# GpSimd drains in the scatter loop of the expert tiles

## The chip, the cores and the metric

The kernel runs on one core of a Trainium2 chip. The metric is device time in microseconds (us) of one execution. The engines are named as the profile names them: PE (TensorE, with PEld for its weight loads), DVE (VectorE), ACT (ScalarE), POOL (GpSimd) and SP (SyncE, which here only issues DMAs). POOL also issues DMAs, and all those whose rows are chosen by a list of indices (DMA_INDIRECT) come from it.

## What is computed

The reference is one transformer layer on x of 4 x 1024 x 256 in f32: a layer norm, a causal attention, a second attention with 16 heads, and a feed-forward part with routed experts. The change is in the last part, which per token is

```python
h = _swiglu(flat @ W1_shared)
routed = jnp.zeros_like(shared)
for e in range(E):
    routed = routed + h @ W2_experts[e] * w[:, e:e + 1]
out = x + (shared + routed).reshape(Bb, Tt, C)
return _rmsnorm(out, norm2_w)
```

with 8 experts, of which w is non-zero for two per token (both of one group of four). The kernel's output is x plus the causal attention plus this.

## The kernel before

Four stages follow one another: `project`, `causal_attention`, `head_attention` and `feed_forward`. Each is a block in which every engine has its own program. At the end of a block each engine executes a DRAIN, then all meet at a barrier; semaphores are then cleared, with two more POOL drains and a barrier for each such clearing (lines 69 and 70). The DRAINs of the block ends stand in the trace under the line that opens the block: L296, L677, L1545 and, for `feed_forward`, L1938.

`feed_forward` has two parts. First come 8 chunks of 512 tokens: hidden values, gates, shared expert, and rows of all tokens written to DRAM (`hidden_d` with the hidden values, `rows_d` with hidden values, base and rest in rows of 1040 f32). In this part POOL sends the tokens to their places in the lists of the 12 pairs of experts, 4 indirect DMAs a chunk, so 32, and gathers the lists back with one more (L1159).

The second part, from some 1280 us to the end, works off 43 expert tiles of 128 tokens (`TILES`, line 31); the tokens of one tile have the same two experts. Tile t passes through these steps, each on its engine:

- POOL gathers its rows from `rows_d` into one of 8 slots (`gather`, L1957, recorded at L1960). For the first 6 tiles the hidden values are gathered once more ahead of that (`gather_early`, L1954), from `hidden_d`.
- PE turns it (`turn_tile`, L2114: 4 transposes), which waits for the gather's landing.
- ACT rounds it (`tile_high`, L2182), DVE takes the rest (`tile_low`, L2251).
- PE multiplies it by its two experts (`experts`, L2130: 24 matmuls).
- DVE adds the weighted sums to the base (`sums`, L2259), ACT squares (L2189) and takes the root (L2195), DVE scales and finishes (`final`, last instruction L2277, which raises `fin_done`).
- POOL scatters the 128 finished rows to the output (`scatter`, L1963, recorded at L1965), once `fin_done` is t + 1.

The order on each engine is written out by hand. PE runs turn(t + 1) ahead of experts(t). DVE runs, in step t: tile_low(t + 1), sums(t - 1), final(t - 2), mean_square(t - 1). So final(t - 3) stands behind tile_low(t), and tile_low(t) behind turn(t). POOL issues gathers 0 to 5, then

```python
for t in range(TILES):
    scatter(t)
    if t + AHEAD < TILES:
        gather(t + AHEAD)
```

with `AHEAD` = 6, so that gather(t + 6) stands behind scatter(t), and from t = 37 on there are only scatters. A gather into a slot that has been used waits for the landing of the scatter two tiles back (`out_sent`). After the loop POOL (L1994) and SP (L2061) wait for the landing of all scatters, and the block ends. Counted out of the program, POOL issues 32 + 1 + 6 + 43 + 43 = 125 DMAs in this block, 21 in the block before it and 38 in `causal_attention`; none in `project`.

Of the kernel before, what the change touches and what calls it, by code (L numbers as in the profile page):

```python
# [30 lines left out]
TILES = N // P + CLASSES - 1  # L31
# [53 lines left out]
class HeadInputs:  # L85
# [3 lines left out]
    RING = 3  # L89
    AHEAD = RING - 1  # L90
    LOADS = 2 * NT * SIDES
    PLACE = PAIRS * S * 4

    def __init__(self, nc, ctx, q_d, k_d, vh_d):
        self.dram = (q_d, k_d, vh_d)
        self.nc = nc
        base = -(-nc.sbuf_base // 32) * 32
        self.base, self.all = base, ctx.enter_context(nc.sbuf_tensor("h_place", [P, 2 * self.AHEAD * PAIRS * S], F32))
        assert nc.sbuf_base == base + 2 * self.AHEAD * self.PLACE
        at = lambda name, i, dt: nc.alloc_sbuf_tensor_at(name, [P, PAIRS, S], dt, offset=base + i * self.PLACE)  # L100
        self.q6 = [at(f"h_q{r}", 2 * r, F32R) for r in range(self.AHEAD)]
        self.k6 = [at(f"h_k{r}", 2 * r + 1, F32R) for r in range(self.AHEAD)]
        self.spares = [at(f"h_spare{i}", i, F32) for i in range(2 * self.AHEAD)]
        self.vh = []
# [1742 lines left out]
def feed_forward(nc, inputs, heads, ya_d, ffw, routing, rows_d, hidden_d, out):  # L1847
# [5 lines left out]
    with ExitStack() as ctx:  # L1853
# [84 lines left out]
        with nc.Block() as block:  # L1938

            @block.gpsimd  # L1940
            def _(pool):
                def whole_ya(c):
                    pool.wait_ge(routing.xn_in, (c + 1) * 16)
                    pool.wait_ge(ya_in[c % 2], (c // 2 + 1) * 16)
                    theirs = rows[c % 2][:, :, REST:REST + D]
                    nc.gpsimd.tensor_tensor(theirs, theirs, xn[:, :, :], ALU.add).then_inc(ya_whole, 1)

                def low_parts(c, i):
                    pool.wait_ge(h_rounded, c * KH + i + 1)
                    nc.gpsimd.tensor_tensor(h[LO][:, i, :], whole[i % 2], h[HI][:, i, :].bitcast(F32),  # L1950
                                            ALU.subtract).then_inc(h_split, 1)

                def gather_early(t):
                    pool.indirect_dma_start(early[t], None, hidden_d,  # L1954
                                            bass.IndirectOffsetOnAxis(listed[:, t:t + 1], 0)).then_inc(early_in[t], 16)

                def gather(t):  # L1957
                    if t >= SLOTS:
                        pool.wait_ge(out_sent[t % SLOTS], t // SLOTS * 16)
                    pool.indirect_dma_start(slot(t), None, rows_d, bass.IndirectOffsetOnAxis(listed[:, t:t + 1], 0))\  # L1960
                        .then_inc(row_in[t % SLOTS], 16)

                def scatter(t):  # L1963
                    pool.wait_ge(fin_done, t + 1)
                    pool.indirect_dma_start(out, bass.IndirectOffsetOnAxis(listed[:, t:t + 1], 0), base(t), None,  # L1965
                                            bounds_check=N - 1, oob_is_err=False).then_inc(out_sent[t % SLOTS], 16)

                for c in range(NCH):
                    routing.send(pool, c)
                    for i in range(KH):  # L1970
                        low_parts(c, i)
                        if i == 1 and c == LASTS:
                            routing.gather_lists(pool)
                    if WHOLE <= c + 1 < NCH:
                        whole_ya(c + 1)
                pool.wait_ge(*fills.released(("LISTS", 0)))
                pool.wait_ge(zeros_stored, 2 * 16)
                for s in range(2):
                    pool.wait_ge(hidden_stored[s], NCH * 16)
                for t in range(EARLY):  # L1980
                    if early[t] is whole[0]:
                        pool.wait_ge(h_split, NCH * KH)
                    gather_early(t)
                pool.wait_ge(rest_stored, NCH * 16)
                pool.wait_ge(rows_stored, NCH * 16)
                AHEAD = SLOTS - 2
                for t in range(AHEAD):
                    gather(t)
                for t in range(TILES):
                    scatter(t)  # L1990
                    if t + AHEAD < TILES:
                        gather(t + AHEAD)
                for s in range(SLOTS):
                    pool.wait_ge(out_sent[s], len(range(s, TILES, SLOTS)) * 16)  # L1994
# [409 lines left out]
```

## Time and profile before

| | |
|---|---|
| median of 3 runs | 1465.1 us (1464.88 to 1467.75) |
| profiled execution, its own time | 1463.6 us |
| its span, first to last instruction | 1461.9 us |
| mean granted TensorE clock | 0.972 |
| PE / DVE / ACT / POOL busy | 1380.3 / 1136.0 / 854.8 / 371.9 us |
| last scatter issued / span ends | 1450.0 / 1461.9 us |

The span is what the profile covers; 1.7 us of the execution lie outside it. Busy time is the time in which an engine executes instructions that the profile counts; a drain is a sequencer instruction and not counted as busy. In a row of the timeline the columns are start and duration in us, engine, line, operation, output<-inputs, shapes and count, and in brackets how long the engine had been idle and what released it.

### The profile page before, as it was taken

Reading aid. Unit: us, or ns where it says so; the run is one execution under the profiler, and the core shown is the slowest. Engines: PE = TensorE matmul, PEld = TensorE weight load, DVE = VectorE, ACT = ScalarE, POOL = GpSimd, SP = SyncE. Lnnn points to the kernel's source line nnn. Section 1 sums busy time; section 2 is a strip of 40 time slices with the busy share of each in tenths; the row PEclk is TensorE's granted clock in tenths of the full one; section 3 lists DMA queues with packets and bytes.
Section 4 is the critical chain, followed back from the end, with each engine's and each line's share of the span. In section 5 each row is a group of like instructions: output and inputs, shape, how many; then the busy total and the mean of one; then the engine's idle time right before and its main releaser. Section 6 shows DMA issues by size and latency. Waiting matters only on the chain. (4 is left out here: it accounts for less than half of the span.)

```text
span 1461.9 us, 26960 instructions
## 1 busy us (share of the span) xinstructions
PE 1380.3 (94%) x9749; PEld 816.1 (56%) x9749; DVE 1136.0 (78%) x1803; ACT 854.8 (58%) x1573; POOL 371.9 (25%) x368
## 2 busy tenths in 40 slices
PE   6999799979999999999999999989999999989995
PEld 3655577734333333333333333335888888789985
DVE  3786575588999999999999999924677776657764
ACT  2445443304888888888888888885334343323332
POOL 0344294045241000000000000101233333355553
PEclk9999999957999999999999999999999999999998
DMA  5799769351443344443322234213565654365551
GB/s 188 266 320 342 250 224 249 71 98 59 91 109 67 44 67 66 67 67 60 67 55 51 46 58 67 75 59 47 166 161 153 175 152 132 88 217 177 176 174 62
DMA packets 119746, 185.06 MB, mean 127 GB/s; under 512 B 26614, under 2 KB 74122, under 8 KB 119622
## 3 DMA queue, kind: packets, MB, share of 16 engines
q1 hardware_dynamic: 94341, 124.55, 34.6%
q0 software_dynamic: 14816, 45.19, 10.4%
q10 hardware_dynamic: 10464, 13.64, 3.1%
q8 instruction: 82, 1.34, 0.4%
q14 instruction: 43, 0.34, 0.1%
HBM read 102.36 MB, written 81.88 MB: 126 GB/s over the span
## 5 line engine op out<-in xcount | busy, mean ns | idle before, releaser
L1799 DVE TENSOR_REDUCE i_saT<-h_banks 128x2 f32<-128x1024 f32 x512 | 617.8, 1221 | 24.9 <-PE h_banks L1668 17.1
L1768 ACT ACTIVATE h_p<-h_banks 128x512 f32<-128x512 f32 x1024 | 551.2, 598 | 137.3 <-PE h_banks L1687 121.9
L1708 PE MATMUL h_po<-h_p,h_v 128*32 128x256 f32 (+1 forms) x3728 | 318.4, 413 | 3.5 <-ACT h_p L1768 1.4
L1687 PE MATMUL h_banks<-h_q,h_k 50*128 50x512 f32 x1024 | 254.4, 495 | 11.7 <-ACT h_p L1768 6.0
L1668 PE MATMUL h_banks<-h_k,h_q 48*128 48x512 f32 x1024 | 222.8, 431 | 10.7 <-DVE i_saT L1799 6.8
L1687 PEld LDWEIGHTS h_banks<-h_q,h_k 50*128 50x128 f32 x1024 | 95.8, 183 | 235.0 <-ACT h_p L1768 190.4
L1708 PEld LDWEIGHTS h_po<-h_p,h_v 128*32 128x32 f32 x3728 | 73.4, 108 | 170.7 <-issue 83.8
L2130 PE MATMUL f_ob<-w_experts,f_h 128*128 x1032 | 146.4, 291 | 1.3 <-issue 0.2
L2130 PEld LDWEIGHTS f_ob<-w_experts,f_h 128*128 128x128 f32 x1032 | 129.9, 191 | 10.3 <-issue 8.1
L1564 POOL COPY h_v<-h_values 128x512 f32<-128x512 f32 x14 | 8.6, 612 | 459.4 <-DMA h_values<-vh_d 459.4
L1668 PEld LDWEIGHTS h_banks<-h_k,h_q 48*128 48x128 f32 x1024 | 101.1, 194 | 38.4 <-DVE i_saT L1799 28.0
L2176 ACT ACTIVATE h_v<-f_pair 128x512 f32<-128x512 f32 x64 | 38.2, 597 | 131.2 <-PE f_pair L2079 131.1
L2079 PE MATMUL f_pair<-w_routed,r_x1p 128*128 128x512 f32 x384 | 93.7, 400 | 2.1 <-PEq L70 2.1
L2079 PE MATMUL f_pair<-r_x1p,w_shared 128*128 128x512 f32 x384 | 92.9, 396 | 2.3 <-DVE f_rows L2238 2.3
L2079 PEld LDWEIGHTS f_pair<-w_routed,r_x1p 128*128 128x128 f32 x384 | 72.6, 191 | 18.3 <-issue 3.0
L2079 PEld LDWEIGHTS f_pair<-r_x1p,w_shared 128*128 128x128 f32 x384 | 71.3, 187 | 19.8 <-DVE f_rows L2238 3.1
L2238 DVE TENSOR_TENSOR h_place<-h_v,f_pair 128x512 f32<-128x512 f32 x48 | 32.9, 686 | 50.1 <-ACT h_v L2176 49.8
L746 PE MATMUL a_sc<-c_kT,c_qT 128*128 128x512 f32 (+3 forms) x192 | 68.3, 493 | 2.3 <-PEq L296 2.3
L1950 POOL TENSOR_TENSOR f_h<-h_place,f_h 128x512 fp32r<-128x512 f32 x32 | 43.8, 1368 | 98.6 <-ACT f_h L2169 97.0
L2251 DVE TENSOR_TENSOR f_h<-f_pair,f_h 128x512 fp32r<-128x512 f32 x43 | 29.7, 692 | 49.0 <-ACT f_h L2182 49.0
L308 POOL TENSOR_TENSOR h_spare<-h_spare,t_sin 128x512 f32<-128x512 f32 x28 | 41.9, 1530 | 101.3 <-DVE h_spare L184 101.3
L773 PE MATMUL a_out<-a_v,a_pT 128*128 128x256 f32 x432 | 63.6, 298 | 0.0
(266 smaller groups left out, 1695.5 us busy)
## 6 DMA issues: line engine op xcount, KB each, us to landing
h_q<-q_d SPq DMA_DIRECT2D x84, 128.0 KB, 5.9
h_k<-k_d SPq DMA_DIRECT2D x84, 128.0 KB, 7.0
ot_d<-h_o ACTq DMA_DIRECT2D x32, 256.0 KB, 2.9
q_d<-t_parts SPq DMA_DIRECT2D x12, 512.0 KB, 5.0
k_d<-t_parts SPq DMA_DIRECT2D x12, 512.0 KB, 5.1
p_xin<-in_L_attn_x SPq DMA_DIRECT2D x8, 512.0 KB, 5.1
xn_d<-p_xn SPq DMA_DIRECT2D x8, 512.0 KB, 5.1
xnT_d<-p_xnT SPq DMA_DIRECT2D x8, 512.0 KB, 6.0
```

The costliest lines, as they stand in the source:

```text
L308: last = nc.gpsimd.tensor_tensor(swap[:, j, :], swap[:, j, :], sin[:, s, :], ALU.mult)
L746: ins = nc.tensor.matmul(sc[u % 2][:, c:c + w], qT[b % 2][:, k, i * P:(i + 1) * P], kT[b % 2][:, k, c:c + w], start=k == 0, stop=k == KD - 1)
L773: ins = nc.tensor.matmul(out[u % 2][:, 0:D], pT[u % 2][left][:, j, :], vp[b % 2][right][:, j, :], start=j == 0 and n == 0, stop=j == i and ...
L1668: ins = nc.tensor.matmul(bank_of(("SLOT", slot), g), q6[r][at, p, i * P:(i + 1) * P], k6[r][at, p, half * CH:(half + 1) * CH], start=True, ...
L1687: ins = nc.tensor.matmul(bank_of(key, g), k6[r][at, p, j * P:(j + 1) * P], q6[r][at, p, c * CH:(c + 1) * CH], start=True, stop=True)
L1708: ins = nc.tensor.matmul(po[h * VW:(h + 1) * VW, at], vh[n % RING][:, j, h, :], probs[u % PR][:, h, at], start=j == 0 and (part == 0 or la ...
L1768: nc.scalar.activation(probs[u % PR][:, h, :], bank_of(("PAIR", f // SIDES), f % SIDES), ACT.Exp, scale=DH ** -0.5).then_inc(exp_done, 1)
L1799: nc.vector.tensor_reduce(halfmax[n % 2][:, m, :], both_banks(("SLOT", slot)), AX.X, ALU.max)\
L1950: nc.gpsimd.tensor_tensor(h[LO][:, i, :], whole[i % 2], h[HI][:, i, :].bitcast(F32), ALU.subtract).then_inc(h_split, 1)
L2079: ins = nc.tensor.matmul(ps[:, half, :], left, right, start=n == 0, stop=n == len(terms) - 1)
L2130: ins = nc.tensor.matmul(to, h[left][:, t % KH, k * P:(k + 1) * P], w2s[right][:, bass.ds(e, 1), k, :], start=k == 0 and n == 0, stop=k == ...
L2176: nc.scalar.activation(sil[f % 2], fills.buffer(key)[:, 0, :], ACT.Silu).then_inc(sil_done[f % 2], 1)
```

## The change

Three lines are added to POOL's loop over the tiles. Ahead of the scatters of tiles 0, 4, 8, ..., 40 and of tile 42 POOL executes a drain: 12 in all. Nothing is removed or moved, and no other engine's program differs.

```diff
@@ -1984,9 +1984,12 @@
                 pool.wait_ge(rest_stored, NCH * 16)
                 pool.wait_ge(rows_stored, NCH * 16)
                 AHEAD = SLOTS - 2
+                DRAINED = 4
                 for t in range(AHEAD):
                     gather(t)
                 for t in range(TILES):
+                    if t % DRAINED == 0 or t == TILES - 1:
+                        pool.drain()
                     scatter(t)
                     if t + AHEAD < TILES:
                         gather(t + AHEAD)
```

## Rows read from the trace of the kernel before

**Rows 1.** Busy time by stretch: us, PE, PEld, DVE, ACT, POOL, PEclk, DMA share, GB/s.
```profile
1280.00:1290.00 10.00, 6.25 (x34) 5.68 (x33) 2.87 (x6) 1.20 (x2) 7.65 (x8) 0.69 0.72 219
...
1300.00:1440.00 140.00, 136.28 (x1056) 126.59 (x1054) 99.20 (x266) 48.74 (x153) 75.10 (x76) 1.00 0.54 172
```

**Rows 2.** Waits from 1300 to 1440 us: total us, times, longest.
```profile
PE f_pair L2114 <- DMA f_rows<-rows_d,r_listed: 2.3, 3, 1.2
```

**Rows 3.** Timeline, all engines, gather 6 to gather 9.
```profile
1301.58 0.98 POOL L1960 DMA_INDIRECT f_rows<-rows_d,r_listed  x1 [0.30 <-issue]
...
1305.72 0.66 PE L2114 MATMUL f_pair<-h_v,f_rows 128*128 128x128 f32 x4 [0.64 <-DMA f_rows<-rows_d,r_listed]
...
1306.52 0.58 ACT L2182 ACTIVATE f_h<-f_pair 128x512 fp32r<-128x512 f32 x1
...
1307.13 0.69 DVE L2251 TENSOR_TENSOR f_h<-f_pair,f_h 128x512 fp32r<-128x512 f32 x1 [0.75 <-ACT f_h L2182]
...
1307.74 0.99 DVE L2259 SCALAR_TENSOR_TENSOR f_rows<-f_ob,f_rows 128x256 f32<-128x256 f32 x2
...
1309.36 0.42 DVE L2277 TENSOR_TENSOR h_place<-h_place 128x256 f32<-128x256 f32 x1
...
1310.62 1.02 POOL L1965 DMA_INDIRECT out_dram<-h_place,r_listed  x1 [1.17 <-DVE h_place L2277]
...
1311.94 0.97 POOL L1960 DMA_INDIRECT h_place<-rows_d,r_listed  x1 [0.30 <-issue]
```

**Rows 4.** Line 1960, all 43 gathers: time from issue to landing.
```profile
DMA to landing us min/median/max: 4.1/4.3/6.9
```

**Rows 5.** Line 1965, all 43 scatters: time from issue to landing.
```profile
DMA to landing us min/median/max: 2.1/2.5/4.2
```

**Rows 6.** Timeline of POOL: gather 5, scatter 0, gather 42, scatters 39 to 42.
```profile
1293.84 0.94 POOL L1960 DMA_INDIRECT f_rows<-rows_d,r_listed  x1 [0.30 <-issue]
1300.23 1.04 POOL L1965 DMA_INDIRECT out_dram<-h_place,r_listed  x1 [5.44 <-DVE h_place L2277]
...
1434.07 0.97 POOL L1960 DMA_INDIRECT h_place<-rows_d,r_listed  x1 [0.30 <-issue]
...
1443.60 0.99 POOL L1965 DMA_INDIRECT out_dram<-f_rows,r_listed  x1 [2.69 <-DVE f_rows L2277]
1445.76 0.98 POOL L1965 DMA_INDIRECT out_dram<-h_place,r_listed  x1 [1.18 <-DVE h_place L2277]
1448.48 1.08 POOL L1965 DMA_INDIRECT out_dram<-h_place,r_listed  x1 [1.74 <-DVE h_place L2277]
1449.95 0.98 POOL L1965 DMA_INDIRECT out_dram<-h_place,r_listed  x1 [0.40 <-issue]
```

**Rows 7.** POOL's drains by line: ns min/median/max, first and last start us.
```profile
L1938 POOLq DRAIN  x1: 7978/7978/7978, 1452.4 to 1452.4; - x1
...
L1545 POOLq DRAIN  x1: 1775/1775/1775, 989.2 to 989.2; - x1
...
L677 POOLq DRAIN  x1: 3172/3172/3172, 269.1 to 269.1; - x1
...
L296 POOLq DRAIN  x1: 4799/4799/4799, 140.5 to 140.5; - x1
...
L69 POOLq DRAIN  x4: 93/118/218, 294.8 to 1461.3; - x4
...
L70 POOLq DRAIN  x4: 34/43/46, 295.7 to 1461.6; - x4
```

**Rows 8.** Packets of POOL's DMA queue: 148 to 270, 295 to 1000, 1003 to 1461 us.
```profile
q0 software_dynamic: 2784, 8.92, 29.6%
...
q0 software_dynamic: 2240, 7.55, 3.7%
...
q0 software_dynamic: 9792, 28.72, 19.6%
```

**Rows 9.** Timeline of POOL around the drain of L296.
```profile
139.24 5.95 POOL L308 TENSOR_TENSOR h_spare<-h_spare,t_sin 128x512 f32<-128x512 f32 x4 [10.32 <-DVE h_spare L184]
```

## The prediction

> **What bounds the kernel now.** I read the busy times by stretch first, then the waits of the tile stage, then the timeline of one turn of its loop, and last the drains. From 1300 to 1440 us PE is busy 136.28 of 140 us at the full 2.4 GHz level [rows 1]: the tile stage is PE's, so long as its tiles come in time. They come barely in time. The waits show that PE stood before a tile's transposes for a gather only 3 times for long, 2.3 us in all [rows 2], but that says nothing of the slack of the other tiles, and the timeline does. Gather 6 is issued at 1301.58 and its transposes wait for it until 1305.72. From there the reader can follow one turn of a loop [rows 3]: transposes of tile 6, ACT's rounding, DVE's tile_low(6), sums(4), final(3) ending at 1309.78, scatter(3) at 1310.62, gather(9) at 1311.94. That turn carries three tiles and takes 1311.94 - 1301.58 = 10.36 us when the gather is what ends it. From gather 6 to gather 42, 36 tiles take 1434.07 - 1301.58 = 132.5 us [rows 3, 6], so 3.68 us a tile and 11.04 for three. The loop through POOL is thus within 0.7 us per three tiles of being the bound itself. POOL is only half busy (75.10 of 140 us [rows 1]), yet whatever delays a scatter delays the gather behind it, and soon PE.
>
> The other place is the end. The last scatter is issued at 1449.95 and takes some 2.1 us to land, but the span goes on to 1461.9. Most of that is one instruction: POOL's drain of the block's end, 7.98 us from 1452.4 [rows 6, 7].
>
> **What a drain costs.** Three drains behind blocks with POOL DMAs took 3.17, 1.78 and 7.98 us, with 2784, 2240 and 9792 packets on POOL's queue in the blocks [rows 7, 8]: 1.1, 0.8 and 0.8 ns a packet, or 83, 85 and 64 ns a DMA at 38, 21 and 125 DMAs. It does not follow what lies further back, for the second is shorter than the first; and drains that follow another take 34 to 218 ns. So a drain goes through each DMA issued since the last one, though the program had waited for all of them beforehand. It also waits: the drain of L296, with no DMA before it, began at 140.5 behind queued POOL work and took 4.80 us, to 145.3, when that work had ended at 139.24 + 5.95 = 145.19 [rows 7, 9]; about 0.1 us after.
>
> What no row shows is a drain with DMAs in flight, and in the loop there are always some. The two ends: it returns at once for them (8 DMAs of 64 ns, 0.5 us, inside POOL's idle 1.17 us before a scatter [rows 3]), or it waits until the youngest has landed. I take the second. The nearest rows are these drains themselves: one waits for older work, and one that visits each DMA has little else to look for than whether it is done.
>
> **The sum.** One drain in the loop, ahead of scatter t: the youngest DMA is gather(t + 5). It lands 4.3 us after its issue at the median [rows 4], the drain ends 0.1 later, and then scatter(t) needs what it needs after any release: from the end of final(3), 1309.78, to the start of scatter(3), 0.84 us [rows 3]. Gather(t + 6) follows the scatter by 1.32 [rows 3]. Gather to gather: 4.3 + 0.1 + 0.84 + 1.32 = 6.6 us, where the pace was 3.68. POOL's earlier idle time is no cover, because the tiles that follow cannot make up the loss before the next drain: gather(t + 9), the youngest before drain t + 4, hangs on gather(t + 6) through the three-tile turn. That turn is 10.36 with a landing of about 4.1; with 4.3 it is 10.6. So four tiles take 6.6 + 10.6 = 17.2 us instead of 4 x 3.68 = 14.7: 2.5 us a drain. Between gather 6 and gather 42 lie nine such rounds (drains 4 to 36): +22.3 us.
>
> Drain 0 has some 45 DMAs to go through (about 3 us) and waits for gather 5: issued at 1293.84, landing up to 6.9 us later, 1300.7. Scatter 0 goes out at 1301.6 instead of 1300.23: +1.4 us [rows 4, 6], passed on at once because gather 6 was waited for. Drain 40 waits for scatter 39 alone; scatter 40 comes at least 2.1 + 0.1 + 0.84 = 3.1 us after it, where it was 2.16, and 0.9 us later is made good before scatter 41, 2.7 us on [rows 5, 6]. Drain 42 waits for scatter 41: 3.1 us instead of 1.47, +1.7 us that nothing behind it hides. The drain at the end then has one DMA to visit instead of 125: it falls from 7.98 to 0.2 us, a gain of 7.8. Nothing else is added: SP only waits for the landings, and the scatters themselves are the same.
>
> Together: 22.3 + 1.4 + 1.7 - 7.8 = **+17.6 us**. Against the profiled execution, 1463.6, that is 1481.2; the median of the runs lies 1.5 above it, so 1482.7, and I say 1482.5.
>
> The Trainium skill ("VectorE: DVE Perf Modes", section "The DRAIN you can't avoid") speaks of the drains of preamble and postamble as about 12 ns each, constant, on all engines. By that there would be no 7.8 us to gain and the sum would be some +25. The trace disagrees for POOL: 34 ns to 7.98 us [rows 7].
>
> **The range.** Downwards: the 0.84 us could be mostly sequencer work that overlaps the wait, as little as 0; 0.8 x 11 drains = 9 us less, 1473.5. Upwards: 0.5 us instead of 0.1 between landing and the drain's end adds 4.4 us; landings in the upper part of 4.1 to 6.9 add another few; and PE's gap of 2.5 us in each round may cost clock: from 1280 to 1290 PE was busy 6.25 of 10 us and the granted clock was 0.69, between the levels of 2.4 and 1.2 GHz [rows 1]. The transposes on the loop, 0.66 us, could at worst double, 6 us in nine rounds. Not all of these come together: 1492.
>
> **Rivals.** First, on the other side: the drain does not wait for DMAs in flight. Its price in the loop is then 0.5 us in POOL's idle 1.17, and nothing moves up to drain 42, which stands directly between scatters 41 and 42 and costs 0.2 to 0.5. The gain at the end stays: -7.8 + 0.4 = -7.4 us, 1457.7. The point that decides is drain 4: does it end before or after gather 9 has landed? For it speaks that every drain of the trace found its DMAs done, so that going through them may be bookkeeping only; against it, the drain that waited for older work. A rule of the Trainium skill points this way ("Perfetto Trace Analysis", section "DMA Instruction — SWDGE (GPSIMD)"): an indirect DMA's record ends when the last descriptor is written, not when the data has moved, and a drain that waits for older instructions would be done with it there. No row here shows whether a drain holds to that. I give it 0.11.
>
> Second: the drain waits as I say, but the end keeps its 7.98 us, because what is gone through are all DMAs of the block and not those since the last drain. Then it is 17.6 + 7.8 = +25.4, 1490.5, and more if each drain in the loop grew with it. Against it stand the short drains behind others and the fall from 3.17 to 1.78 us while the DMAs of the whole program rose [rows 7]. 0.08.
>
> Third: a DMA counts as done well ahead of its landing. If a drain step were 5.1 us instead of 6.6, a round would take 15.7, 1.0 more than before, nine rounds 9 us, and gain and loss would about meet: 1465. There is no row for it but the gap between the first rival and the forecast. 0.04.
>
> **How the numbers follow.** The forecast has 0.77, the rivals 0.11, 0.08 and 0.04. Some 0.2%, 2.9 us, is what a measurement can tell from no change. Slower are the forecast and the second rival, 0.85; within it the third, 0.04; faster the first, 0.11. The range from 1473 to 1492 holds the forecast's cases and the second rival; it leaves out the first and the third, and about 0.05 at its ends.
>
> **What would show it.** In the timeline of POOL: gathers 10, 14, ..., 42 start some 6.6 us after the one before them, the other gathers follow quickly; the drains of the loop are 2 to 3.5 us long and each ends just after the landing of the youngest gather. In PE's waits, line 2114 stands for a gather some nine or ten times, over 2 us each, where it was 2.3 us in all. The drain of L1938 is about 0.2 us and the span ends some 2 us after the last landing. The forecast is wrong if the loop's drains end before those landings (then the first rival), if the last drain is still several us (the second), or if scatter(t) starts at once behind the drain's end (then the low end of the range).

## The result and the profile after

The changed kernel takes 1493.57 us (1490.9 to 1494.48, 4 runs) against 1466.21 us (1464.88 to 1467.75, 4 runs) for the kernel before on the same chip: ratio 1.0174, 95% interval 1.0150 to 1.0199, so 25.5 us slower. Here and below, a change in us is the ratio's excess over 1 times the median of before; the plain difference of the two medians is 27.4 us. The forecast was 17.4 us. The profiled execution has a span of 1492.4 us.

The stage ahead of the tiles does not always take the same time: gather 5, which lies ahead of the change and of all edits below but the drains in the chunks, is issued at 1293.84 us in the trace of before and at 1297.67 in that of after, and between 1294 and 1302 in the others. So stretches are counted from there. From the issue of gather 5 to the span's end it was 1461.9 - 1293.84 = 168.1 us, and it is now 1492.4 - 1297.67 = 194.7: +26.6 us. Four pieces make it up, each read off POOL's timeline:

| piece | before | after | change | forecast |
|---|---|---|---|---|
| gather 5 to gather 6 (drain 0) | 7.74 | 10.96 | +3.2 | +1.4 |
| gather 6 to gather 42 (drains 4 to 36) | 132.49 | 160.89 | +28.4 | +22.3 |
| gather 42 to scatter 42 (drains 40 and 42) | 15.88 | 18.79 | +2.9 | +1.7 |
| scatter 42 to the end | 11.95 | 4.09 | -7.9 | -7.8 |

POOL's timeline of after at the points that bound these pieces [rows 6]:

```profile
1297.67 0.95 POOL L1960 DMA_INDIRECT f_rows<-rows_d,r_listed  x1 [0.30 <-issue]
1307.28 1.04 POOL L1965 DMA_INDIRECT out_dram<-h_place,r_listed  x1 [8.66 <-DVE h_place L2280]
1308.63 0.98 POOL L1960 DMA_INDIRECT f_rows<-rows_d,r_listed  x1 [0.30 <-issue]
...
1318.95 1.03 POOL L1965 DMA_INDIRECT out_dram<-h_place,r_listed  x1 [4.11 <-DVE h_place L2280]
1320.28 0.97 POOL L1960 DMA_INDIRECT h_place<-rows_d,r_listed  x1 [0.31 <-issue]
1325.81 1.03 POOL L1965 DMA_INDIRECT out_dram<-f_rows,r_listed  x1 [4.56 <-issue]
1327.14 0.98 POOL L1960 DMA_INDIRECT h_place<-rows_d,r_listed  x1 [0.30 <-issue]
...
1337.68 0.97 POOL L1960 DMA_INDIRECT f_rows<-rows_d,r_listed  x1 [0.30 <-issue]
1343.34 1.10 POOL L1965 DMA_INDIRECT out_dram<-h_place,r_listed  x1 [4.68 <-issue]
1344.74 0.98 POOL L1960 DMA_INDIRECT f_rows<-rows_d,r_listed  x1 [0.30 <-issue]
...
1469.52 0.98 POOL L1960 DMA_INDIRECT h_place<-rows_d,r_listed  x1 [0.30 <-DVE f_rows L2280]
...
1485.20 1.07 POOL L1965 DMA_INDIRECT out_dram<-h_place,r_listed  x1 [1.86 <-DVE h_place L2280]
1488.31 0.98 POOL L1965 DMA_INDIRECT out_dram<-h_place,r_listed  x1 [2.04 <-issue]
```

The block in the middle is one drained round. Gather 9 is issued at 1320.28, then the drain stands, and only at 1325.81 does scatter 4 go out, with gather 10 behind it at 1327.14: 6.9 us from gather to gather, where 3.7 was the pace. Gather 13 follows gather 10 after 10.54 us, which is the turn through PE, ACT, DVE and POOL of [rows 3], and then comes the next drained step, 7.06 us. "issue" as the releaser of the drained scatters means that nothing which the profile counts ended the wait; the drain is not counted.

POOL's drains of after [rows 7]; first the one ahead of scatter 4, then all twelve, then the one at the block's end:

```profile
L1992 POOLq DRAIN  x1: 5791/5791/5791, 1319.2 to 1319.2; - x1
...
L1992 POOLq DRAIN  x12: 2522/5802/13233, 1293.2 to 1485.0; - x12
...
L1938 POOLq DRAIN  x1: 126/126/126, 1490.7 to 1490.7; - x1
```

Drain 4 ends at 1324.96. Gather 9's landing stands in the trace at 1324.60. All nine drains from 4 to 36 end 0.36 to 0.37 us after the last landing. The drain at the end has shrunk from 7978 to 126 ns.

PE's waits for gathers in after, from 1300 to 1475 us [rows 2]:

```profile
PE f_pair L2117 <- DMA f_rows<-rows_d,r_listed: 16.4, 5, 4.5
...
PE f_pair L2117 <- DMA h_place<-rows_d,r_listed: 11.6, 5, 2.7
```

These are ten waits of some 2 to 4.5 us, 28.0 us in all, where 2.3 was the sum of three. They fall on tiles 6, 10, ..., 42, whose gathers stand behind a drained scatter. PE's timeline of after around one of them:

```profile
1325.80 0.60 PE L2117 MATMUL f_pair<-h_v,h_place 128*128 128x128 f32 x4
1326.15 3.07 PE L2133 MATMUL f_ob<-w_experts,f_h 128*128 x24
1331.53 0.66 PE L2117 MATMUL f_pair<-h_v,h_place 128*128 128x128 f32 x4 [2.31 <-DMA h_place<-rows_d,r_listed]
1331.95 4.82 PE L2133 MATMUL f_ob<-w_experts,f_h 128*128 x24
```

Behind the gap PE's 24 expert matmuls take 4.82 us instead of 3.07. The busy times by stretch say why, in the columns of [rows 1]: in the 3.5 us behind that gap the granted clock is 0.55, mostly the lower level of 1.2 GHz, and over the tile stage it is 0.87 where it was 1.00.

```profile
1308.00:1470.00 162.00, 135.97 (x1002) 133.28 (x1003) 94.06 (x252) 44.98 (x144) 73.28 (x74) 0.87 0.48 146
...
1332.00:1335.50 3.50, 3.46 (x18) 3.21 (x17) 2.53 (x7) 1.11 (x3) 1.05 (x2) 0.55 0.77 267
```

### The profile page after: what moved, and what is told of

The parts are those of the page before. It is cut to its first block and busy times, and to the rows that moved or that the text cites. A ratio compares the mean times of both kernels' runs of the same rounds, so it can differ in the third digit from the quotient of the medians.

```text
span 1492.4 us, 26972 instructions
## 1 busy us (share of the span) xinstructions
PE 1393.2 (93%) x9749; PEld 832.5 (56%) x9749; DVE 1137.6 (76%) x1803; ACT 853.7 (57%) x1573; POOL 371.9 (25%) x368
## 3 DMA queue, kind: packets, MB, share of 16 engines
q0 software_dynamic: 14816, 45.19, 10.6%
## 5 line engine op out<-in xcount | busy, mean ns | idle before, releaser
L1687 PE MATMUL h_banks<-h_q,h_k 50*128 50x512 f32 x1024 | 255.0, 496 | 11.7 <-ACT h_p L1768 6.0
L2133 PE MATMUL f_ob<-w_experts,f_h 128*128 x1032 | 151.7, 308 | 0.2
L2133 PEld LDWEIGHTS f_ob<-w_experts,f_h 128*128 128x128 f32 x1032 | 142.7, 214 | 1.8 <-issue 1.6
```

The lines of the kernel that those rows point to most:

```text
L1687: ins = nc.tensor.matmul(bank_of(key, g), k6[r][at, p, j * P:(j + 1) * P], q6[r][at, p, c * CH:(c + 1) * CH], start=True, stop=True)
L2133: ins = nc.tensor.matmul(to, h[left][:, t % KH, k * P:(k + 1) * P], w2s[right][:, bass.ds(e, 1), k, :], start=k == 0 and n == 0, stop=k == ...
```

## The experiments

Each time is against runs of the kernel before on the same chip. Its medians there were 1468.4 us (the first four experiments), 1471.8 (the next four) and 1471.4 (the last three). Theory W is: a drain waits for the landing of the youngest DMA in flight, and that wait goes round the gather loop to PE.

**Waiting without draining.** The drains are replaced by waits on the semaphore of the youngest DMA.

```diff
+                def youngest(t):
+                    if t + AHEAD - 1 < TILES:
+                        u = t + AHEAD - 1
+                        pool.wait_ge(row_in[u % SLOTS], (u // SLOTS + 1) * 16)
+                    else:
+                        pool.wait_ge(out_sent[(t - 1) % SLOTS], ((t - 1) // SLOTS + 1) * 16)
                 for t in range(TILES):
+                    if t % 4 == 0 or t == TILES - 1:
+                        youngest(t)
                     scatter(t)
```

> No drain; at the same twelve places POOL waits on the semaphore of the youngest DMA it has issued (gather t + 5; for t = 40 and 42 the scatter before). Theory W (the loss is the wait for the landing, passed on through the gather loop): the tiles slow down almost as in the changed kernel, gather 6 to gather 42 some 155 us instead of 132.5, and the drain at the end keeps its 8 us, so +24 to +30 us against the kernel before. Rival P (the loss is work that the drain does on POOL, going through its list): a wait without that work costs little, at most +5 us.

Measured: 1493.74 us, ratio 1.0181 (1.0152 to 1.0211), +26.6 us. Its waits from 1300 to 1480 us:

```profile
POOL out_dram L1965 <- DMA f_rows<-rows_d,r_listed: 24.9, 5, 7.1
POOL out_dram L1965 <- DMA h_place<-rows_d,r_listed: 20.6, 5, 4.3
...
PE f_pair L2122 <- DMA f_rows<-rows_d,r_listed: 13.5, 5, 3.2
PE f_pair L2122 <- DMA h_place<-rows_d,r_listed: 11.2, 5, 2.7
```

Its drain at the end:

```profile
L1938 POOLq DRAIN  x1: 7978/7978/7978, 1481.9 to 1481.9; - x1
```

POOL now waits openly for ten gathers, 5, 9, ..., 41, and PE for the ten that stand behind these waits, 6, 10, ..., 42. Gather 6 to gather 42 takes 158.65 us, against 160.89 with drains and 132.49 without either. So most of the 28.4 us is the wait for the landing, and rival P falls. How much the drain's own work adds is not read from the difference of 2.2 us, since the same nine rounds took 2.3 us more in another execution (the version without the last two drains, below). It is read at each round: from the landing of the youngest gather to the start of the scatter it is 0.82 us here and 1.21 with a drain, so 0.39 us a round, 3.5 in nine.

**One tile more of lead.** The change, with gathers running 7 tiles ahead.

```diff
-                AHEAD = SLOTS - 2
+                AHEAD = SLOTS - 1
                 for t in range(TILES):
+                    if t % 4 == 0 or t == TILES - 1:
+                        pool.drain()
```

> The changed kernel, but gathers run 7 tiles ahead instead of 6. Theory W says that a drain costs because PE needs each gather within half a microsecond of its landing; one tile more of lead (3.7 us) covers a drain step that is 3.2 us longer. Then gather 6 to gather 42 falls to some 140 us, and the kernel to -5 to +3 us against the one before, the short drain at the end included. Rival C (PE is slow because its granted clock drops or because POOL is overloaded, whatever the lead): still +15 us or more.

Measured: 1468.76 us, ratio 1.0015 (0.9993 to 1.0037). No difference from the kernel before is left that stands clear of the noise, with the same twelve drains in place. Gather 6 to gather 42 takes 144.65 us, more than the 140 expected; drain 0 now lies in this piece too. PE's waits for gathers in its tile stage are down from 28.0 to 8.3 us:

```profile
PE f_pair L2116 <- DMA h_place<-rows_d,r_listed: 5.1, 4, 2.4
...
PE f_pair L2116 <- DMA f_rows<-rows_d,r_listed: 3.2, 4, 1.6
```

So most of the cost is one of lead: it is the slack between a gather's landing and its tile's turn that decides. Rival C, which had +15 us or more, falls. But the drains are not free even so, for the longer lead without drains gains by itself (**Lead alone**, below). From gather 5 to the end this kernel takes 169.4 us and that one 162.7. With the 7.8 us that the end gives back, the drains cost 14.5 us at this lead, where they cost 34.5 at the shorter one. POOL itself is now near its limit: between drains it issues a gather every 2.6 us, most without any wait, and a drained step takes 6.7 to 7.6 us.

**One drain, late.** Ahead of scatter 38, behind the last gather.

```diff
                 for t in range(TILES):
+                    if t == TILES - 5:
+                        pool.drain()
```

> One drain alone, ahead of scatter 38, when the last gather has been issued and nothing on PE waits for POOL any more. Theory W: the drain waits for gather 42 and goes through some 120 DMAs (5 us), scatters 38 to 41 go out late but close together, scatter 42 is late by 0 to 1.5 us, and the drain at the end falls from 8.0 to 0.3 us: -5 to -8 us against the kernel before. Rival S (what the drain at the end costs is a fixed price of a block's end, not of the DMAs since the last drain): the end keeps 8 us, 0 to +2 us.

Measured: 1461.67 us, ratio 0.9960 (0.9947 to 0.9972), -5.9 us, faster than the kernel before. Its two drains:

```profile
L1991 POOLq DRAIN  x1: 8832/8832/8832, 1440.1 to 1440.1; - x1
...
L1938 POOLq DRAIN  x1: 458/458/458, 1457.5 to 1457.5; - x1
```

The 8.8 us lie beside PE's last tiles, and the end pays for 5 DMAs instead of 125. Scatter 42 follows gather 42 by 17.26 us instead of 15.88, so 1.4 us of the gain is lost. Rival S falls: what the end costs depends on the DMAs since the last drain.

**One drain, too late.** Ahead of scatter 42 alone (`t == TILES - 1`).

> One drain alone, ahead of scatter 42. Theory W: the same list of 124 DMAs is gone through, but now between the last two scatters, so what the end gains is lost there: 5 to 8 us later scatter 42, 7.8 us shorter end, together -2 to +2 us. If the pass in the loop were free, -6 us.

Measured: 1469.18 us, ratio 1.0016 (0.9990 to 1.0041): no difference. The last two scatters in POOL's timeline:

```profile
1452.95 1.08 POOL L1965 DMA_INDIRECT out_dram<-h_place,r_listed  x1 [1.84 <-DVE h_place L2279]
1462.75 0.98 POOL L1965 DMA_INDIRECT out_dram<-h_place,r_listed  x1 [8.72 <-issue]
```

Its two drains:

```profile
L1991 POOLq DRAIN  x1: 9213/9213/9213, 1452.7 to 1452.7; - x1
...
L1938 POOLq DRAIN  x1: 131/131/131, 1465.2 to 1465.2; - x1
```

Between the two scatters lie 9.8 us instead of 1.47, and the end is 7.8 us shorter. The work is moved, not saved.

**Half as many drains.** `t % 8 == 0 or t == TILES - 1`.

> The change with drains ahead of tiles 0, 8, 16, 24, 32, 40 and 42: four drained rounds with gathers in flight instead of nine, ten with drain 0 counted instead of five. Theory W: what a drain takes is not won back, because the loop through POOL is no quicker than PE between drains, and it adds once per drain: some 3 us each, so gather 6 to gather 42 some 145 us against 132.5 and 161, and +8 to +13 us against the kernel before. Rival K (the loss is caught up when there is more time between drains): gather 6 to gather 42 stays near 133 to 136 us, and the kernel is at -3 to +2 us.

Measured: 1485.77 us, ratio 1.0090 (1.0064 to 1.0116), +13.2 us, at the upper edge of what was expected. Gather 6 to gather 42 takes 151.1 us, above the 145 expected: 4.65 us for each of the four drains, where the nine drains of the change cost 3.16 each. One of the four drained steps, in POOL's timeline:

```profile
1339.70 0.97 POOL L1960 DMA_INDIRECT f_rows<-rows_d,r_listed  x1 [0.30 <-issue]
1346.46 1.02 POOL L1965 DMA_INDIRECT out_dram<-h_place,r_listed  x1 [5.78 <-issue]
1347.79 0.97 POOL L1960 DMA_INDIRECT f_rows<-rows_d,r_listed  x1 [0.30 <-issue]
```

So little is won back between drains, and rival K falls; but each drain costs more. Most of that is the drained step itself, from gather to gather 8.09, 7.42, 8.04 and 7.22 us, where it is 6.9 on average in the change. The drain now goes through sixteen DMAs and not eight, so that the scatter starts 1.54 us after the landing instead of 1.21, and two of the four gathers that were waited for landed only after 5.2 us, for a reason that was not looked for. The rest is an echo, also of drain 0, which the last experiment shows.

**Drains only where POOL has time.** Ahead of `routing.send` for chunks 1 to 7, once ahead of the early gathers (behind the gather of the lists), and ahead of scatter 38.

> Drains only where POOL has time: ahead of the sends of chunks 1 to 7, behind the gather of the lists, and ahead of scatter 38. Theory W: the first eight find their DMAs landed and POOL idle and cost nothing; the drain ahead of scatter 38 has some 87 DMAs to go through instead of 120 (4.4 us instead of 6.2 after the last landing), so that scatter 42 is no later than its rows: -6.5 to -8.5 us against the kernel before, 1 us below the single drain ahead of scatter 38. If those first drains hold up the sends, it is slower than that one.

Measured: 1462.78 us, ratio 0.9948 (0.9930 to 0.9965), -7.7 us. The drain ahead of scatter 38 ended 5.7 us after the last landing and not 4.4; the gain over the single late drain is within the intervals. The seven drains ahead of the sends began while earlier work of POOL still ran and ended 0.4 us after it.

**Lead alone.** The kernel before with `AHEAD = SLOTS - 1`, no drains.

> The kernel before with gathers 7 tiles ahead, no drains. Theory W: PE's few waits for gathers (2.3 us) go and little else changes: -1 to -3 us. If the gathers now wait for the scatter that frees their slot, 0 to +2.

Measured: 1464.69 us, ratio 0.9943 (0.9922 to 0.9964), -8.4 us, where -1 to -3 was expected; from gather 5 to the end 162.7 us instead of 168.1. That is more than the waits of [rows 2] promise. From the transposes of tile 6 to those of tile 42 PE takes 128.7 us instead of 133.1, and it waits for no gather of `rows_d` any more. What else makes up the difference is open.

**Both.** `AHEAD = SLOTS - 1`, the drains ahead of the sends and behind the gather of the lists, and one ahead of scatter 37.

> Gathers 7 ahead, drains ahead of the sends, behind the gather of the lists and ahead of scatter 37. Theory W: the gains add: -8 to -11 us against the kernel before; scatter 42 no later than its rows, the drain at the end under 0.5 us.

Measured: 1458.02 us, ratio 0.9902 (0.9880 to 0.9924), -14.4 us, more than the -8 to -11 expected; from gather 5 to the end 155.5 us.

**Both, without the drains ahead of the sends.**

```diff
-                AHEAD = SLOTS - 2
+                AHEAD = SLOTS - 1
                 for t in range(TILES):
+                    if t == TILES - 6:
+                        pool.drain()
```

> Gathers 7 ahead and one drain ahead of scatter 37, none ahead of the sends. Theory W: that drain has some 120 DMAs to go through instead of 86, but five scatters' time to do it in, so it is hidden all the same and the result is that of the version with the drains ahead of the sends: from gather 5 to the end 155 to 157 us (168.1 before), -9 to -13 us. If the drains ahead of the sends were worth something, some 1 us or more above that.

Measured: 1458.29 us, ratio 0.9913 (0.9889 to 0.9937), -12.8 us; from gather 5 to the end 155.6 us. The drains ahead of the sends show no gain that these runs can tell. This is the version to keep: two small edits that beat both kernels. Its POOL timeline from the last gather on:

```profile
1432.54 0.98 POOL L1960 DMA_INDIRECT h_place<-rows_d,r_listed  x1 [0.30 <-issue]
1434.73 1.02 POOL L1965 DMA_INDIRECT out_dram<-f_rows,r_listed  x1 [1.21 <-DVE f_rows L2279]
1444.10 1.01 POOL L1965 DMA_INDIRECT out_dram<-f_rows,r_listed  x1 [8.35 <-issue]
1445.41 0.99 POOL L1965 DMA_INDIRECT out_dram<-f_rows,r_listed  x1 [0.31 <-issue]
...
1451.62 0.98 POOL L1965 DMA_INDIRECT out_dram<-h_place,r_listed  x1 [0.40 <-issue]
```

Its drain at the end:

```profile
L1938 POOLq DRAIN  x1: 539/539/539, 1454.0 to 1454.0; - x1
```

The drain holds back scatter 37 to 1444.10, scatters 38 to 40 follow at 1.3 us each, and scatter 42 goes out as soon as scatter 41 has been issued, as before.

**Without the last two drains.** The change with drains 0, 4, ..., 36 alone.

> The change without its drains 40 and 42. Theory W: the rounds stay as they are (gather 6 to gather 42 some 161 us); the last scatter follows gather 42 by some 17 us instead of 18.8, and the drain at the end has the 8 DMAs since drain 36 and takes 0.5 us instead of 0.13: 1 to 2 us below the changed kernel, +23 to +27 us against the one before.

Measured: 1497.57 us, ratio 1.0182 (1.0141 to 1.0222), +26.8 us, and not 1 to 2 us below the changed kernel. The pieces concerned came out as expected: gather 42 to scatter 42 takes 16.6 us (18.8 with those drains), the drain at the end 0.70 us (0.5 expected). The total does not show it: the rounds took 163.2 us in this execution instead of 160.9, and the interval is 12 us wide.

**Drain 0 alone.**

> Drain 0 alone. Theory W: it waits for gather 5 and then goes through 45 DMAs (1.9 us): from gather 5 to gather 6 some 11 us instead of 7.7, passed on whole to the end of the tiles; the drain at the end has 80 DMAs less the six gathers instead of 125 and falls by 2 to 3 us: 0 to +2 us against the kernel before.

Measured: 1474.69 us, ratio 1.0024 (1.0005 to 1.0044), +3.5 us; a miss. Gather 5 to gather 6 takes 11.3 us, as expected, but gather 6 to gather 42 then takes 136.8 us instead of 132.5, and the drain at the end still 6.58 us. PE's timeline of the stall and what follows:

```profile
1314.81 1.11 PE L2116 MATMUL f_pair<-h_v,f_rows 128*128 128x128 f32 x4 [4.38 <-DMA f_rows<-rows_d,r_listed]
1315.57 4.98 PE L2132 MATMUL f_ob<-w_experts,f_h 128*128 x24
1320.39 0.60 PE L2116 MATMUL f_pair<-h_v,f_rows 128*128 128x128 f32 x4
1320.74 3.07 PE L2132 MATMUL f_ob<-w_experts,f_h 128*128 x24
...
1332.00 0.66 PE L2116 MATMUL f_pair<-h_v,h_place 128*128 128x128 f32 x4 [1.65 <-DMA h_place<-rows_d,r_listed]
...
1333.18 4.27 PE L2132 MATMUL f_ob<-w_experts,f_h 128*128 x21 [0.18 <-issue]
```

The busy times of the two stretches behind gaps, in the columns of [rows 1]:

```profile
1313.00:1320.00 7.00, 5.19 (x25) 5.20 (x26) 2.61 (x7) 1.31 (x4) 2.97 (x3) 0.51 0.78 242
...
1333.00:1337.00 4.00, 3.82 (x20) 3.83 (x20) 2.61 (x7) 1.00 (x4) 1.27 (x3) 0.57 0.67 229
```

Its drain at the end:

```profile
L1938 POOLq DRAIN  x1: 6582/6582/6582, 1466.5 to 1466.5; - x1
```

The one stall of 4.38 us has an echo: tile 10 is waited for as well, 1.65 us. And behind each of the two gaps PE's clock is near the lower level for some microseconds, so that a tile's experts take 5.0 us instead of 3.1. Where drains come every four tiles, PE waits for the next gather anyway and this is hidden; where one comes alone or every eight tiles, PE has no such slack and it can show.

No run was made to separate lateness and clock, but the trace of the version with half as many drains sets them side by side. Behind drains 8 and 16 PE stood for almost the same time, 3.12 and 2.98 us; the clock fell after the first gap only:

```profile
1352.20:1357.20 5.00, 4.89 (x27) 4.69 (x27) 2.61 (x7) 1.31 (x4) 1.63 (x3) 0.66 0.77 218
1386.00:1390.00 4.00, 3.82 (x31) 3.43 (x30) 2.61 (x7) 1.25 (x4) 1.36 (x2) 1.00 0.77 233
```

After the first gap the experts took 4.95 us and gather 18 came 5.15 us after gather 17; after the second they took 3.73 us and gather 26 came 3.92 us after gather 25. Drains 24 and 32 give the same pair: 5.40 us where the clock fell, 3.85 where it did not. So in these four cases the echo goes with the clock, 1.2 to 1.6 us of it.

## Why the prediction was right, and where its sizes were off

The forecast was right in its direction and its mechanism, and the measured 25.5 us lie inside the range of +7.9 to +26.9 us that it stood for against the median of 1465.1; its middle was some 8 us too low. That is close to the range's upper end: by the difference of the medians, 27.4 us, it would lie just outside. (The median of these runs itself, 1493.6, lies 1.6 us above the range's upper end; the kernel before was 1.1 us slower in them too.) Of the four pieces, three came out dearer than forecast and the fourth as forecast, so no error hid another. Point by point:

- **The drain waits for DMAs in flight.** No row of before showed it; nine drains that end 0.36 us behind a landing do. The first rival, which the rule on the end of an indirect DMA's record in the Trainium skill ("Perfetto Trace Analysis", section "DMA Instruction — SWDGE (GPSIMD)") would favour, is out: the record of gather 9 had ended at 1321.25, the drain at 1324.96. The rule itself agrees with the trace, where gather 9's record ended 3.35 us ahead of its landing; but a drain does not go by it.
- **The loop passes it on.** Three-tile turns of 10.4 to 11.7 us, 11.0 on average, and drained steps of 6.7 to 7.2 us, 6.9 on average, alternate, where 10.6 and 6.6 were forecast. The waits without drains and one tile more of lead show the cause.
- **The step that failed is "the drain ends 0.1 later".** It took the going through the DMAs to be done while the youngest was waited for. It comes behind: 0.36 us for 8 DMAs, 1.88 for the 45 of drain 0. At drain 0 that is the whole miss, +3.2 instead of +1.4. In each round it is 0.26 of the 0.68 us by which a round cost more than forecast (3.16 instead of 2.48). The range had allowed 0.5 us for it.
- **The landings were mis-sized too.** In the sum they were 4.3 us; the median of all 43 gathers is now 4.5 ("4.1/4.5/6.9" from issue to landing). A round holds two of them: the one that the drain waits for, 4.34 us on average, and the one behind the drained scatter, 4.51. That is about 0.25 of those 0.68 us; the rest lies in small parts along the turn.
- **The tail.** Drain 42 cost what was forecast: scatter 42 follows scatter 41 by 3.11 us (3.1 forecast, 1.47 before). The other 1.3 us lie between gather 42 and scatter 41. There PE had waited 2.1 us for gather 42, the granted clock was then 0.50 for over 3 us, and the experts of tile 41 took 4.96 us instead of 3.63. The range had the clock in it, the sum had not.
- **The end.** 7.98 to 0.13 us, as forecast. The second rival is out. The Trainium skill gives about 12 ns for the drains of preamble and postamble, on all engines ("VectorE: DVE Perf Modes", section "The DRAIN you can't avoid"). The drain here stands at the end of a block of the program itself, where POOL's took 7.98 us before and 0.13 after, so that figure does not carry over to it. The prediction's "The trace disagrees" goes too far: no run here shows the drains that the page speaks of.
- **The drains' own length** was given as 2 to 3.5 us; it is 5.6 to 6.0 for the nine of the rounds. Their records begin while the scatter before is still being issued, ahead of the gather's record. It changes nothing in the sum, which goes by their ends.

## What to carry to other kernels

In every trace here a GpSimd drain waited for all DMAs that GpSimd had in flight, so its place mattered more than its count: put it where no engine needs the next DMA soon. Before moving work to an engine that is "half busy", follow one turn of the loop through it; here POOL's idle time was no slack, since the gathers of tiles 6 to 42 landed half a microsecond ahead of their use at the median and 1.4 us at most, in the 33 whose landing the trace gives. Where that is so, one more tile of lead may be worth more than the work that was to be hidden: lead and one well-placed drain gave -12.8 us, the twelve drains +25.5.

## What the runs showed of the hardware that was not expected

- **A drain's price has two parts.** Where it had to wait, it ended after the last landing by 0.12 us with 2 DMAs since the last drain, 0.24 with 5, 0.36 with 8, 0.69 with 16 and 1.88 with 45: 0.04 to 0.06 us each. Where all had landed before it began, it took 0.13 us for one, 0.46 for 5, 0.54 for 6, 0.70 for 8, 1.78 for 21, 3.17 for 38 and 6.58 for 80: about 0.08 each beyond the first. The 125 of the block's end, 32 of them small sends, took 7.98, 0.064 each. Late drains with 86 to 124 DMAs ended 4.8 to 6.8 us after the last landing, without a clear order by count; what sets that is open. A POOL drain did not wait for another engine's DMA: ahead of the send of chunk 1, in the version with drains there, it ended at 1040.08 us while a DMA that SP had issued at 1029.52 landed at 1041.20.
- **A short stall can cost PE twice.** After each of the ten gaps of 2.0 to 4.5 us in the changed kernel the granted clock was at the lower level for some 3 to 7 us, and 24 matmuls then took 4.2 to 5.5 us instead of 3.1. It does not always come: in the version with half as many drains the clock stayed at 1.00 after gaps of 2.98 and 2.02 us, and they took 3.7.
